# A fused cross-attention layer: the product P·V placed four slots behind its scores, and the rest of a sequence one slot sooner

## What is computed

```python
q = x @ Wq + bq;  k = ctx @ Wk + bk;  v = ctx @ Wv + bv          # 16 heads of 32
scores = q @ k^T / sqrt(32);  scores = where(j < i, scores, -1e30)
attn = softmax(scores);  attn[:, :, 0, :] = 0                     # row 0 attends to nothing
x = layer_norm(x + (attn @ v) @ Wo + bo)
out = layer_norm(x + relu(x @ W1 + b1) @ W2 + b2)                 # W1: 512 x 2048
```

## Time and profile before

| | |
|---|---|
| runs | 2654.1, 2656.3, 2656.74 us; median 2656.3 |
| the profiled execution | 2657.87 us |
| its span (first to last instruction) | 2656.1 us |
| PE busy | 2507.3 us, 94% |
| DVE busy | 2098.6 us, 79% |
| ACT busy | 1629.0 us, 61% |
| POOL busy | 1574.0 us, 59% |
| `attention` in steady state | from about 110 to 1100 us of the span |
| the seam with `feed` | about 1100 to 1250 us |
| `feed` | from there to the end |

### The profile page before, as it was taken

How to read it: one execution, slowest core, us unless ns; L and a number is a source line. 1 busy time by engine, 2 the same in 40 slices (tenths; PEclk the granted TensorE clock), 3 DMA queues, 4 the chain that set the end, 5 groups by cost and what they waited for, 6 DMA issues and landing times.

```text
span 2656.1 us, 62863 instructions
## 1 busy us (share of the span) xinstructions
PE 2507.3 (94%) x22664; PEld 1889.3 (71%) x22664; DVE 2098.6 (79%) x4886; ACT 1629.0 (61%) x2881; POOL 1574.0 (59%) x1721
## 2 busy tenths in 40 slices
PE   4899999999999999978999999999999999999998
PEld 1455555555555555557888888888888888888887
DVE  7999999999999999779767677676767676767675
ACT  2788888999999999777343444343434344444433
POOL 2677777777777777656555555454545554454543
PEclk9999999999999999989999999999999999999999
DMA  5444444443343333346131322222222222222220
GB/s 164 113 117 117 116 114 112 113 107 102 96 104 103 105 104 99 86 130 173 49 68 47 68 51 68 53 66 56 61 60 57 65 57 64 57 65 56 65 57 25
DMA packets 444456, 225.04 MB, mean 85 GB/s; under 512 B 302368, under 2 KB 388192, under 8 KB 444144
## 3 DMA queue, kind: packets, MB, share of 16 engines
q1 hardware_dynamic: 442544, 219.71, 32.6%
q10 hardware_dynamic: 1600, 1.31, 0.2%
HBM read 112.36 MB, written 57.69 MB: 64 GB/s over the span
## 4 chain that ended last, share of the span: by engine, by line
PE 59%; POOL 24%; issue 12%; DVE 3%; DMA 1%; SPq 1%; ACT 0%; POOLq 0%; DVEq 0%; ACTq 0%
PE h_ps L1659 25%; POOL prob_lo L495 24%; PE acc L1675 22%; PE front L1645 6%; PE lin_ps L934 2%; PE o_ps L976 1%; PE max_ps L907 1%; PE st_ps L956 1%; PE lin_ps L930 1%; DVE W L1616 1%; POOL scan L510 0%; PE st_ps L991 0%; POOLq L83 0%; PE o_ps L978 0%; SPq L1078 0%
## 5 line engine op out<-in xcount | busy, mean ns | idle before, releaser
L495 POOL TENSOR_TENSOR prob_lo<-probs,prob_hi 128x512 f16<-128x512 f32 (+1 forms) x768 | 792.5, 1039 | 348.2 <-ACT prob_hi L582 314.9
L1659 PE MATMUL h_ps<-x_halves,W 128*128 128x256 f16 x6144 | 754.9, 273 | 3.6 <-ACT hf L1444 3.6
L1675 PE MATMUL acc<-W,hs 128*128 128x256 f16 x5376 | 669.6, 273 | 0.0
L1659 PEld LDWEIGHTS h_ps<-x_halves,W 128*128 128x128 f16 x6144 | 595.9, 98 | 88.4 <-issue 16.0
L1444 ACT ACTIVATE hf<-h_ps,b1s,scale_evac 128x256 f32<-128x256 f32 x512 | 284.6, 562 | 568.6 <-PE h_ps L1659 568.1
L1675 PEld LDWEIGHTS acc<-W,hs 128*128 128x128 f16 x5376 | 526.0, 98 | 60.9
L1369 POOL TENSOR_TENSOR hf<-hf 128x256 f32<-128x256 f32 x256 | 241.2, 942 | 493.4 <-ACT hf L1444 493.1
L588 ACT ACTIVATE probs<-st_ps,exp_scale 128x512 f32<-128x512 f32 (+1 forms) x768 | 467.1, 608 | 104.2 <-PE st_ps L991 84.4
L886 DVE CUSTOM_DVE_ANT_0 max_ps<-max_ps,mask_q 128x256 f32<-128x256 f32 (+2 forms) x768 | 419.1, 561 | 85.4 <-PE max_ps L907 84.6
L582 ACT ACTIVATE prob_hi<-probs 128x512 f16<-128x512 f32 (+1 forms) x768 | 427.3, 556 | 22.4 <-issue 7.2
L1612 DVE TENSOR_TENSOR hs<-hf,hs 128x896 f16<-128x896 f32 x256 | 281.2, 1118 | 143.6 <-ACT hs L1433 143.6
(11 more groups left out here) (152 smaller groups left out, 3540.9 us busy)
## 6 DMA issues: line engine op xcount, KB each, us to landing
heads<-stage SPq DMA_DIRECT2D x748, 64.0 KB, 2.1
raw_c<-in_cT SPq DMA_DIRECT2D x64, 256.0 KB, 3.2
raw_x<-in_xT SPq DMA_DIRECT2D x64, 256.0 KB, 4.4
o_in<-ctx_rows SPq DMA_DIRECT2D x256, 64.0 KB, 2.5
x_in<-in_x SPq DMA_DIRECT2D x32, 512.0 KB, 4.0
x_rows<-x SPq DMA_DIRECT2D x64, 256.0 KB, 2.1
o_in<-x_rows SPq DMA_DIRECT2D x256, 64.0 KB, 2.4
out<-y SPq DMA_DIRECT2D x32, 512.0 KB, 3.0
```

The costliest lines, as they stand in the source:

```text
L495: pool.tensor_tensor(prob_lo[:, k % 4, 0:w], probs[:, k % PROBS, 0:w], prob_hi[:, k % 4, 0:w], ALU.subtract).then_inc(pl_done, 1)
L1659: last = pe.matmul(h_ps[:, f % 2, 0:T], W1[:, aw, j, f * P:(f + 1) * P], x1_halves[:, item.parity, aa, j, :], start=(j == 0 and m == 0), s ...
L1675: last = pe.matmul(acc_products[:, n, :], hs[:, p % HS, aa, n, :], W2[:, p, aw, n, :], start=(p == 0 and m == 0 and n % 2 == 0), stop=(p = ...
```

## The change

`PV_AT` is `ST_AT + 4` where it was `ST_AT + 3`, and `LIN` with all that is set from it, the loads of x, the looks, the ranges and the splits stand one slot sooner. Since `ST_AT` is one less and `PV_AT` one more relative to it, `PV_AT` keeps its slot, 93, and V's last products and stores stay within the 143 slots. `FEED_AFTER` is one less, too. The loads of c (slots 0 to 3) and the steps on W1 and W2 keep their slots.

```diff
-    LOAD = {"c": (0, 1, 2, 3), "x": (3, 6, 9, 12)}
-    LOOK = {"c": (9, 11), "x": (16, 20)}
-    TOPS = 21
-    SPREAD = 22
-    GATHER = 26
-    RANGE = 31
-    SPLIT = {"c": 36, "x": 48}
+    LOAD = {"c": (0, 1, 2, 3), "x": (2, 5, 8, 11)}
+    LOOK = {"c": (8, 10), "x": (15, 19)}
+    TOPS = 20
+    SPREAD = 21
+    GATHER = 25
+    RANGE = 30
+    SPLIT = {"c": 35, "x": 47}
     SPLIT_STEP = 3
-    LIN = 48
+    LIN = 47
     OUT = LIN + 4
     MAX_AT = LIN + 25
     ROW_AT = MAX_AT + 11
     ST_AT = ROW_AT + 6
-    PV_AT = ST_AT + 3
+    PV_AT = ST_AT + 4
...
-FEED_AFTER = 46
+FEED_AFTER = 45
```

## The result

The changed kernel takes **2691.8 us** (median of 4 runs, 2687.0 to 2693.1) beside 2656.5 us for the kernel before: a ratio of 1.0134, with a 95% interval of 1.0121 to 1.0147. It is 35 us slower, where 11 us less had been forecast, and it lies outside the range of 2627 to 2667 us. The profiled execution of the changed kernel took 2687.0 us with a span of 2685.1, so 29 us more than the execution profiled before.

A forecast was written before the change was run, and what follows sets the result against it. PE, ACT and DVE were taken as all near their limit, each leading in a stretch. V's -15, the rows' +5 and the seam's -1 summed to -11 us, giving 2645 us on the scale of the runs' median, range 2627 to 2667 us.

The forecast's parts named there:

- c's loads keep slots 0 to 3: On SP, one of c's loads falls behind the twelve head moves; the splits use c 35 slots later, so booked 0.
- V four slots behind: In `attention`, PE's waits for `prob_lo` ahead of V go: 1.0 us a sequence, -15 us, between 0 and -27.
- Rival 1: ACT, DVE and PE each lead in a stretch and V's waits only hide theirs: no gain, 2656 us, chance 0.20.
- rival 3: DVE's splits of x (L596) start behind a running `prob_lo`, each up to 0.4 us longer: 2665 to 2677 us, chance 0.25.
- The rows behind the stores of W2: In early sequences SP issues the rows of maxima later; PE's wait grows 0.75 us in seven periods: +5 us, up to +11.
- early period: Sequence time while W2's blocks are summed and stored: 70.4 to about 70.2 us; over 1.6 us growth means rows undersized.
- late period: Sequence time without W2's sums and stores beside the attention: to fall from 67.9 to about 66.9 us.
- The turn of parity: On PE and DVE, maxima pair the other way and `osum` changes slots: 0, bounds 0.9 us a sequence each way.
- The seam: Where `attention` meets `feed`, PE waits 12.2 us for `prob_lo`; booked -1 us, bounds -6 and +2.
- `feed`: The stretch in which no product P·V is left; the change was booked at 0 there.

The follow-up runs named there:

- V alone: Kernel before with only V moved, to four slots behind its scores (PV_AT = ST_AT + 4): 2654.8 us, ratio 1.0005.
- the last comparison: Changed kernel with c's loads in slots 0, 0, 1, 2 and W1 and W2 steps a slot sooner (2660.7 us, 1.0020), set against V alone (1.0005).
- V back: Changed kernel with V three slots behind its scores again (PV_AT = ST_AT + 3), all else as changed: 2693.1 us, ratio 1.0151.

## Why the prediction was wrong

**The step that failed** is "c's loads keep slots 0 to 3: one of them falls behind the twelve head moves instead of ahead. The splits use c 35 slots later. 0." It named the transfer that is passed, and then the wrong consumer. Long before the splits DVE looks at c, in slots 8 and 10, and the change moved that look sooner in the same edit. "They move with the projection that they serve … so that nothing between them changes" holds for x, whose loads moved, and not for c. The trace before had the facts. DVE was idle for 0.19 us ahead of the second half of the look, so there was no slack at all, with a full DVE around it. Ahead of the first half it was not idle, but the second load was issued 10.4 us before it (718.69 and 729.14 us) and takes 3.2 us at the median to land, so the room of some 7 us is less than the twelve moves take, 8.87. The term was booked at 0 and is worth 33 us: 1.0134 falls to 1.0009 when c's loads alone are put right. In the kernel before the same order around c costs 23 us; the other 12 come only together with the rest of the change. The terms don't add: 32, 33 and 19 us are each won back by one edit (the look, c's loads, the steps on W1 and W2), and why they overlap so no run takes apart. The sum by what was measured is 0 for V, 33 for c's loads and 2 for all the rest.

**V four slots behind, -15 us.** The waits at L976 for `prob_lo` went as forecast and the time did not: V alone measures 1.0005, so this term was mis-sized by its whole 15 us. Rival 1's outcome is right; its mechanism, waits that only hide others, is one of two that the traces allow, beside rival 3's below. I had argued against it with the 0.6 us a sequence that fall where ACT is not full, and had looked for the next limit in each engine's busy share; PE's waits for the maxima, already the larger in the earlier trace rows, grew by 39 us.

**The rows behind the stores of W2, +5 us.** Moved alone this gains 5 us, so the sign was wrong: I followed POOL's one `prob_lo` and not what SP has to issue meanwhile. In the changed kernel the same place costs much more than booked, about 19 us with c late (with all the steps on W1 and W2 moved) and nothing with c in time. The forecast said that an early period grown by over 1.6 us would show the rows undersized. It grew by 2.5 us, from 70.1 to 72.6, and either edit alone, c's loads or the steps on W1 and W2, brings it back to 70.0, so the growth took both. The late period has no such stores and grew by 2.1; there only c's loads help (68.2, against 70.1 with the steps sooner).

**The turn of parity, 0 with bounds of 13 us each way.** Some 4 us by the last comparison, from intervals that overlap; nothing speaks against the bounds.

**Rival 3, the forecast's slower case, at a quarter of the chance.** It got the sign right, but the 35 us are c's loads. Its signs were looked for in the sum: the splits (L596) took 62.3 and 51.4 us before, for x and c, and 51.7 and 65.0 after, 3 us more in 1000 and not 24. The sum hides two opposite moves. The splits of c before:

```profile
L596 DVE SCALAR_TENSOR_TENSOR acts<-raw_c,inverse,acts 128x512 f16<-128x512 f32 x56 | 51.4, 917 | 0.0
```

and in the changed kernel:

```profile
L596 DVE SCALAR_TENSOR_TENSOR acts<-raw_c,inverse,acts 128x512 f16<-128x512 f32 x56 | 65.0, 1161 | 0.0
```

The first comes with V's lag, whatever the parity: 917 to 1195 ns with V alone, 940 to 1161 from the kernel with V back to the changed one. DVE's busy time over the whole execution goes the same way, 2098.6 to 2120.8 us and 2087.9 to 2115.9. Between the gathers it is 1.7 us a sequence with V alone, over the 0.6 from which rival 3 was to decide, and the time stayed level instead of rising. So longer splits, this rival's sign, did come, with V's lag and on c's side; that they met `prob_lo` more often is not shown, and what they cost can't be told from V's hidden gain. The second move needs V's lag and the shift together: x's splits take 1034 ns with V alone, 1123 with V back and 922 with both.

Long times also moved between two small lines that make the rows. In the changed kernel (ns, least/median/most):

```profile
L819 DVE TENSOR_SCALAR negmax_parts<-maxima x56: 338/494/1133, 107.8 to 1087.0; 128x16 f16<-128x16 f32 x56
...
L821 DVE SCALAR_TENSOR_TENSOR negmax_parts<-maxima,negmax_parts x56: 178/179/183, 108.9 to 1087.4; 128x16 f16<-128x16 f32 x56
```

L821 reached 1081 ns before and now never exceeds 183; L819, which took 163 ns at the median before (and 989 at most), now takes 494 at the median. In sum the pair takes 38.3 us in 56 rounds where it took 40.6 in 58. The long times did not go away, they changed place. The Trainium skill, "SBUF — State Buffer", section "Who interferes with whom", names the `tensor_scalar` form, in a fast mode, among those that share their ports with GpSimd, beside the form with two inputs in SBUF, which is L821's, and L819 is a `tensor_scalar`. These rows fit it; no run here shows in which mode L819 ran.

**The seam, -1 us, and `feed`, 0.** Behind the last gather the changed kernel takes 3.1 us less (1629.8 to 1626.7 us), in one execution of each: within the bounds of -6 and +2, and too little to tell from no change.

## What to carry to other kernels

When a schedule moves against some transfers that stay, list every reader of each transfer, not the last or the costliest, and for each read the idle time ahead of it in the trace of before. A read that already has a few tenths of a microsecond of idle time "by issue" on an engine that is full around it has no slack; for a read without idle time, compare when its data landed. Here twelve small transfers ahead of such a read cost more than all the waits that the change was to remove. And a wait inside a ring of engines that are all nearly full needn't be worth its own length: here 20.7 us of waits taken from PE bought nothing, while DVE's own instructions grew longer.

## What was not expected of the hardware

One queue that issues in order carries delays to transfers that have nothing to do with their cause. Each of the twelve head moves (64 KB) holds SP for about 0.64 us (7.69 us for twelve), so a group of them is a gap of 8 us in front of whatever comes next. And the issue at L398 that waits for POOL holds back the rows of maxima, which need nothing from that sum: SP stood from 321.2 to 327.04 us with the rows behind it.

A short pause of PE can cost more than its own length. After the pause of 1.95 us the granted clock fell to 0.50 for some 6 us, and three products of 128x512 at L934 took 1.43 us at that clock where they take 0.81 at 1.00. How much of the changed kernel's 35 us this is no run separates, but the kernel with V back loses as much at a mean clock of 0.990, that of the kernel before.

And the same DVE instructions on the same data can take longer because another engine's work was moved: c's splits went from 917 to 1195 ns on the mean when only V stood a slot later.
